# An adaLN transformer block with a ternary feed-forward on one core: the prologue's loads on two queues, first products by feature halves, and the last group's transpositions and gating reordered

## The chip, the cores and the metric

One core of one Trainium2 chip runs the whole block in one launch. The metric is the device time of one execution in microseconds (us), median over several runs.

## The reference

The input x holds 8 sequences of 128 tokens with 256 features, and a condition vector of 256 features belongs to each sequence. Everything is float32.

```python
ada = (cond @ ada_w + ada_b)[:, None, :]
shift1, scale1, gate1, shift2, scale2, gate2 = split(ada, 6)
x1 = ln(x) * (1 + scale1) + shift1
q, k, v = (x1 @ qkv_w + qkv_b)            # 16 heads of 128
attn = softmax(q k^T / sqrt(128)) v
x = x + gate1 * (attn @ out_w + out_b)
x2 = ln(x) * (1 + scale2) + shift2
x = x + gate2 * (gelu(x2 @ ffn_w1 + ffn_b1) @ ffn_w2 + ffn_b2)
# second block: two products with weights rounded to {-s, 0, s} by groups of 64
h = square(relu(x @ ternary(W_fc).T))
out = x_in + rms_norm(h) @ ternary(W_proj).T
```

`x_in` is the input of the kernel; the hidden width of both feed-forwards is 1024.

## The kernel before

**Tiling.** The eight sequences form two quads of four (512 tokens). Features lie on the partitions in two halves of 128 (`KD = 2`), so an activation tile is 128 x 512 and a matrix product is a series of TensorE instructions with 512 columns into one PSUM bank of eight. For precision each float32 operand is split into a high part and a low part, and a product is three instructions: high by high, high by low, low by high (`split_mm`, L1225 to L1231). ScalarE (ACT) makes the high parts by a copy; VectorE (DVE) or GpSimd (POOL) make the low parts by a subtraction (`x_lo_part` L881, `lo_part` L348 to L350).

**Order of the work.** Every engine has its own instruction list, written out by hand, and the lists meet in counting semaphores. There is no planner. A list runs strictly in its order, so what stands behind a wait waits as well.

- *Prologue.* SP (the block at L289) loads x quad 0 in two halves (`x0_in`), the first part of ada_w, the first head's Q and K weights, four bias vectors, the V weights and the rest. ACT's queue loads the condition and ada_b (L664, L665). TensorE transposes the condition (L1433) and ada_b (L1436), fills waiting time with products of the identity (`keep_awake`, L1425 to L1427), makes the conditioning products (`ada_product`, L1438, L1442), and transposes the normalised quad 0 (`transpose_x`, L1446 to L1464, first quad at L1456) sequence by sequence and then raw x (`transpose_raw`, L1415 to L1423). DVE and ACT then modulate it out of PSUM: DVE feature half 1 (L868), ACT half 0 (L520), four sequences each. `first_query` makes Q of head 0 from the halves as they come, the biases are transposed at L1502, and K (`project`), the first V block (`first_values`, L1489 to L1498) and the scores (L1298) follow. Then come the products of the second head and the transposition of the normalised quad 1 (L1463).
- *Loop.* Sixteen heads in four groups (`NG`) of four; in a group a unit is one head of one quad, eight units (`UG`). For each unit TensorE makes scores, transposes the probabilities, multiplies by the values (`pv`) and by the output weights; DVE finds maxima, ACT takes exponentials, POOL normalises (L391). Projections of coming heads lie between.
- *Last group.* The units are written out (`last_unit` L1385 and DVE's `unit` with `last`). In unit 5 DVE adds the last output product of quad 0 to yT (`accumulate` L969), multiplies by the gate and adds x (`gate_y`, L958 to L967). In unit 6 TensorE transposes yT back (`transpose_y`, L1537 to L1543, instructions on L1541), and the second normalisation begins. Output head by head is split by ACT (`o_hi_part` L532) and DVE (`o_lo_part`, L949 to L953).
- *First feed-forward, quad 0* (L1607 to L1622 on TensorE, L728 to L733 on ACT, L1122 to L1131 on DVE). For each of eight hidden blocks c: TensorE `ffn1`, ACT GELU into one of two buffers (L718) and the high part, DVE the low part (`h_lo_part`, L893). A GELU waits until the low part two blocks earlier is made, since it writes over its buffer; `ffn1` waits for the GELU two blocks earlier, since it writes over its bank. Into this stretch fall quad 1's `accumulate` (L976), `gate_y` (L962, L966), `transpose_y`, the statistics for its normalisation (L814, L833) and the transpositions of the ternary weights (L1581). The second product of the feed-forward follows and in it the transposition of the normalised quad 1 (L1463).
- *Ternary feed-forward* and output at the end.

The wait that orders the transpositions of yT before the change:

```python
def transpose_y(quad):
    pe.wait_ge(gated, quad + 1)
    for s in range(SQ):
        for c in range(KD):
            m = nc.tensor.transpose(bank[BACK[quad][s // 2]][...], yT[:, c, cols(quad, s)], ident[:, :])
    m.then_inc(gt_mm, 1)
```

Of the kernel before, what the change touches and what calls it, by code (L numbers as in the profile page):

```python
# [21 lines left out]
P = 128  # L22
# [3 lines left out]
H = 16  # L26
# [31 lines left out]
def adaln_block(nc, x, cond, ada_w, ada_b, qkv_w, qkv_b, out_w, out_b, ffn_w1, ffn_b1, ffn_w2, ffn_b2,  # L58
                w_fc, w_proj, out):
    ctx = ExitStack()  # L60
    with ctx:
# [125 lines left out]
        x01_hi, xn0_done, xt0_done = sem("x01_hi"), sem("xn0_done"), sem("xt0_done")  # L187
# [152 lines left out]
        def _(pool):  # L340
# [124 lines left out]
            for k in range(KD):  # L465
                wv_lo_part(k, k + 1)
# [24 lines left out]
        def _(act):  # L491
# [15 lines left out]
            def modulate(e, shift, scale, src):  # L507

                quad, xf = e % NQ, xfull if e else xq0
                if e:  # L510
                    act.wait_ge(xt_done, e)
                act.wait_ge(ada_ready, 1 if e < NQ else 2)
                if e >= 1:
                    act.wait_ge(xs_lo, KD * e)
                for s in range(SQ):
                    b = quad * SQ + s
                    if e == 0:
                        act.wait_ge(xt0_done, s // 2 + 1)
                        src = bank[6:8] if s > 1 else (bank[BV], bank[BO])
                    m = nc.scalar.activation(xf[:, 0, s * P:(s + 1) * P], src[0][:, s * P:(s + 1) * P], ACT.Identity,  # L520
                                             bias=ada[:, shift, b:b + 1], scale=ada[:, scale, b:b + 1])
# [3 lines left out]
                if e:  # L525
                    act.wait_ge(mod_d, e + 1)
                    hi_part(x_hi[:, 1, cols(quad)], xfull[:, 1, :], xs_hi)
# [141 lines left out]
            nc.scalar.activation(bias[:, 0:NA], bank[6][:, 0:NA], ACT.Copy).then_inc(small_cp, 1)  # L669
# [5 lines left out]
            act.wait_ge(small_t, 3)  # L675
            nc.scalar.activation(bias[:, NA:NBIAS], bank[4][:, 0:NBIAS - NA], ACT.Copy).then_inc(small_cp, 1)
            nc.scalar.activation(kbias[:, :], bank[4][:, KB - NA:VB - NA], ACT.Copy, scale=SCALE).then_inc(small_cp, 1)
            act.wait_ge(small_cp, 4)
            wqk_hi_part(1, 32)
            keep_k0(0, 1)  # L680
# [120 lines left out]
        def _(dve):  # L801
# [53 lines left out]
            def modulate(e, shift, scale, src):  # L855

                quad, xf = e % NQ, xfull if e else xq0
                if e:
                    dve.wait_ge(xt_done, e)
                dve.wait_ge(ada_ready, 1 if e < NQ else 2)  # L860
                if e:
                    dve.wait_ge(xs_lo, KD * e)
                for s in range(SQ):
                    b = quad * SQ + s
                    if e == 0:
                        dve.wait_ge(xt0_done, s // 2 + 1)
                        src = bank[6:8] if s > 1 else (bank[BV], bank[BO])
# [4 lines left out]
                if e:  # L872
                    split_lo(quad, KD * e)
                else:
                    nc.vector.tensor_copy(x_hi[:, 1, cols(quad)], xf[:, 1, :]).then_inc(x01_hi, 1)
                    dve.wait_ge(x01_hi, 1)
                    x_lo_part(quad, 1, xf)
                    dve.wait_ge(xs_hi, 1)
# [851 lines left out]
```

## Time and profile before

| | us |
|---|---|
| median of 3 runs | 350.53 |
| lowest and highest run | 349.86, 351.02 |
| the profiled execution | 350.69 |
| its span, first to last instruction | 348.9 |
| TensorE busy | 342.3 |
| VectorE busy | 222.4 |
| ScalarE busy | 220.2 |
| GpSimd busy | 148.7 |

Busy times are sums over instructions in the span. PE is TensorE's products and PEld its weight loads, which overlap them; the end of a product is modelled, so the step from the start of one to the start of the next is the better measure of its cost. SPq and ACTq are the instruction queues of SP and ACT when they issue a transfer. The idle time before an instruction stands in square brackets with what released it.

### The profile page before, as it was taken

Reading aid. Unit: us, or ns where it says so; the run is one execution under the profiler, and the core shown is the slowest. Engines: PE = TensorE matmul, PEld = TensorE weight load, DVE = VectorE, ACT = ScalarE, POOL = GpSimd, SP = SyncE. Lnnn points to the kernel's source line nnn. Section 1 sums busy time; section 2 is a strip of 40 time slices with the busy share of each in tenths; the row PEclk is TensorE's granted clock in tenths of the full one; section 3 lists DMA queues with packets and bytes.
Section 4 is the critical chain, followed back from the end, with each engine's and each line's share of the span. In section 5 each row is a group of like instructions: output and inputs, shape, how many; then the busy total and the mean of one; then the engine's idle time right before and its main releaser. Section 6 shows DMA issues by size and latency. Waiting matters only on the chain.

```text
span 348.9 us, 5879 instructions
## 1 busy us (share of the span) xinstructions
PE 342.3 (98%) x1950; PEld 293.7 (84%) x1950; DVE 222.4 (64%) x386; ACT 220.2 (63%) x560; POOL 148.7 (43%) x140
## 2 busy tenths in 40 slices
PE   8999999999999999999999999999999999999995
PEld 7888888889888888888888888888787788889884
DVE  6676756553555664456466454585875788577796
ACT  2773565667576657756664675667579536876593
POOL 3571329736534964644595573479341100000000
PEclk9999999999999999999999999999999999999998
DMA  6953003100300320030020002020000000000002
GB/s 176 362 192 120 3 0 120 62 1 3 120 0 0 120 60 0 0 120 0 25 95 0 0 6 115 0 62 0 4 0 2 0 2 0 0 2 1 1 32 90
DMA packets 12338, 16.53 MB, mean 47 GB/s; under 512 B 720, under 2 KB 8992, under 8 KB 12320
## 3 DMA queue, kind: packets, MB, share of 16 engines
q1 hardware_dynamic: 12136, 16.16, 14.2%
q8 instruction: 10, 0.16, 0.2%
q10 hardware_dynamic: 184, 0.15, 0.1%
q14 instruction: 8, 0.07, 0.1%
HBM read 15.25 MB, written 1.05 MB: 47 GB/s over the span
## 4 chain that ended last, share of the span: by engine, by line
PE 74%; issue 20%; DVE 3%; ACT 1%; POOL 1%; POOLq 0%; ACTq 0%
PE bank L1228 16%; PE bank L1230 16%; PE bank L1229 16%; PE bank L1315 8%; PE bank L1298 8%; PE bank L1304 4%; PE bank L1427 2%; PE bank L1442 1%; DVE yT L976 1%; DVE yT L966 1%; PE bank L1463 1%; PE bank L1422 1%; DVE yT L962 0%; ACT prob L579 0%; ACT hbuf L718 0%
## 5 line engine op out<-in xcount | busy, mean ns | idle before, releaser
L391 POOL TENSOR_TENSOR prob<-prob,rinv 128x512 f32<-128x512 f32 x32 | 36.2, 1131 | 60.3 <-DVE rinv L1025 59.9
L579 ACT ACTIVATE prob<-bank,negmax 128x128 f32<-128x128 f32 x128 | 45.4, 365 | 25.6 <-DVE negmax L1012 25.6
L1315 PEld LDWEIGHTS bank<-probT,vals 128*128 128x128 f32 x256 | 33.3, 191 | 3.2 <-issue 0.8
L952 DVE SCALAR_TENSOR_TENSOR o_lo<-bank,bias,o_hi 128x512 fp32r<-128x512 f32 x32 | 23.9, 745 | 17.2 <-ACT o_hi L532 17.2
L532 ACT ACTIVATE o_hi<-bank,bias 128x512 fp32r<-128x512 f32 x32 | 21.9, 686 | 19.4 <-PE bank L1315 19.4
L1315 PE MATMUL bank<-probT,vals 128*128 128x128 f32 x256 | 33.9, 275 | 0.0
L350 POOL TENSOR_TENSOR wqk_lo<-raw_qk,wqk_hi 128x512 fp32r<-128x512 f32 x16 | 21.2, 1323 | 19.6 <-ACT wqk_hi L493 18.1
L488 POOL TENSOR_TENSOR xr<-raw_qk,xt 128x256 f32<-128x256 f32 x1 | 0.7, 721 | 67.2 <-ACT raw_qk L796 67.2
L1012 DVE TENSOR_REDUCE negmax<-bank 128x4 f32<-128x512 f32 x32 | 21.8, 682 | 7.9 <-PE bank L1298 7.9
L1228 PE MATMUL bank<-wv_hi,x_hi 128*128 128x512 f32 x62 | 26.1, 420 | 0.0
L579 ACT ACTIVATION_READ_ACCUMULATOR prob<-bank,negmax 128x1 f32 x128 | 26.0, 203 | 0.0
L1025 DVE RECIPROCAL rinv<-rowsum 128x4 f32<-128x4 f32 x32 | 5.7, 177 | 31.2 <-ACT prob L579 31.2
L1228 PE MATMUL bank<-o_hi,wo_hi 128*128 128x512 f32 x64 | 25.3, 395 | 0.0
L1230 PE MATMUL bank<-o_hi,wo_lo 128*128 128x512 f32 x64 | 25.0, 390 | 0.0
L1229 PE MATMUL bank<-o_lo,wo_hi 128*128 128x512 f32 x64 | 24.9, 390 | 0.0
L1230 PE MATMUL bank<-wv_hi,x_lo 128*128 128x512 f32 x62 | 24.4, 393 | 0.0
L1229 PE MATMUL bank<-wv_lo,x_hi 128*128 128x512 f32 x62 | 24.2, 390 | 0.0
L1228 PE MATMUL bank<-x_hi,wqk_hi 128*128 128x512 f32 x54 | 24.0, 445 | 0.0
L537 ACT ACTIVATE vals<-bank 128x512 f32<-128x512 f32 x32 | 19.0, 601 | 4.5 <-PE bank L1230 3.4
L1230 PE MATMUL bank<-x_hi,wqk_lo 128*128 128x512 f32 x54 | 21.2, 393 | 0.0
L1229 PE MATMUL bank<-x_lo,wqk_hi 128*128 128x512 f32 x54 | 21.1, 392 | 0.0
L897 DVE COPY probT<-bank 128x512 f32<-128x512 f32 x29 | 19.8, 683 | 2.0 <-PE bank L1304 2.0
(218 smaller groups left out, 974.1 us busy)
## 6 DMA issues: line engine op xcount, KB each, us to landing
raw_qk<-in_L_cond_qkv_w_dram SPq DMA_DIRECT2D x6, 512.0 KB, 4.6
raw_v<-in_L_cond_qkv_w_dram SPq DMA_DIRECT2D x4, 512.0 KB, 4.1
raw_o<-in_L_cond_out_w_dram SPq DMA_DIRECT2D x4, 512.0 KB, 3.5
t_w<-in_L_cond_ada_w_dram SPq DMA_DIRECT2D x1, 1024.0 KB, 8.9
raw_w<-in_L_cond_ffn_w_dram SPq DMA_DIRECT2D x2, 512.0 KB, 6.9
t_raw<-in_L_ffn_W_fc_dram SPq DMA_DIRECT2D x4, 256.0 KB, 3.7
t_raw<-in_L_ffn_W_proj_dram SPq DMA_DIRECT2D x4, 256.0 KB, 3.8
raw_qk<-in_L_cond_ffn_w_dram SPq DMA_DIRECT2D x1, 1024.0 KB, 4.9
```

The costliest lines, as they stand in the source:

```text
L350: nc.gpsimd.tensor_tensor(lo, raw, hi.bitcast(F32), ALU.subtract).then_inc(lo_sem, 1)
L391: nc.gpsimd.tensor_tensor(e, e, rinv[:, j % 2, :].unsqueeze(2).broadcast_to([P, SQ, P]), ALU.mult).then_inc(norm_done, 1)
L532: nc.scalar.activation(hi, psum, ACT.Identity, bias=bias[:, bass.ds(at, 1)]).then_inc(hi_sem, 1)
L579: e = nc.scalar.activation(prob[:, j % 2, s, :], bank[BS][:, s * P:(s + 1) * P], ACT.Exp, bias=negmax[:, j % 2, s:s + 1], accum_out=rowsum ...
L897: nc.vector.tensor_copy(probT[:, :, :].rearrange("p s t -> p (s t)"), bank[BV][:, :]).then_inc(p_done, 1)
L952: nc.vector.scalar_tensor_tensor(out=lo[:, :], in0=bank[BO][:, :], scalar=bias[:, bass.ds(HG * G + VB + j % HG, 1)], in1=hi[:, :].bitcast( ...
L1012: nc.vector.tensor_reduce(negmax[:, j % 2, :], bank[BS][:, :].rearrange("p (s t) -> p s t", s=SQ), axis=AX.X, op=ALU.max, negate=True).the ...
L1228: nc.tensor.matmul(dst, ah, bh, start=start and n == 0, stop=False, skip_group_check=True)
L1229: nc.tensor.matmul(dst, ah, bl, start=False, stop=False, skip_group_check=True)
L1230: m = nc.tensor.matmul(dst, al, bh, start=False, stop=stop and n == len(terms) - 1, skip_group_check=True)
L1298: m = nc.tensor.matmul(bank[BS][:, t], q[:, t], k[:, t], start=True, stop=True)
L1315: m = nc.tensor.matmul(bank[BO][:, s * P:(s + 1) * P], vals[:, b, h], probT[:, s, :], start=True, stop=True)
```

## The change

In the prologue the second half of x quad 0 and the four bias vectors are loaded from ACT's queue, the half of x first of all, and SP waits for the first half of x alone. The biases are transposed together with ada_b into one bank, ahead of the conditioning products, and copied in one go. There are 5, 3 and 1 calls of `keep_awake` where there were 5, 7 and 3, and they stand elsewhere. The first quad is transposed by feature half, half 1 first; both DVE and ACT modulate both halves, DVE sequences 0 and 1, ACT sequences 2 and 3, and each makes the high part of its own two sequences. Q and K of head 0 are made together from the halves. One wv_lo part moves from POOL to DVE, and DVE copies one half of the transposed raw x (`xT`) that ACT copied; ACT's half comes later. In the last group `gate_y` is cut in two (`gate_y` and `add_x`) with a signal for each feature half, and yT is transposed by halves. In the first feed-forward of quad 0, gate and add of quad 1 stand behind low parts 2 and 3, the statistics behind low part 6 instead of 5, and the transposition of yT behind hidden block 6 instead of 5.

```diff
 @block.sync
-            for h in range(2):
-                s = slice(h * SQ // 2, (h + 1) * SQ // 2)
-                sp.dma_start(xt[:, s, :], x[s].rearrange("b t d -> t b d")).then_inc(x0_in[h], 16)
+            sp.dma_start(xt[:, 0:SQ // 2, :], x[0:SQ // 2].rearrange("b t d -> t b d")).then_inc(x0_in[0], 16)
             sp.dma_start(ada_w1, ada_w[:, 0:2 * D].rearrange("(k p) n -> p k n", p=P)).then_inc(ada1_in, 16)
-            sp.wait_ge(x0_in[1], 16)
+            sp.wait_ge(x0_in[0], 16)
...
-            for src, at, n in ((qkv_b, QB, 3 * H), (out_b, OB, KD), (ffn_b1, F1B, NC), (ffn_b2, F2B, KD)):
-                sp.dma_start(brow[at - NA:at - NA + n, :], src.rearrange("(n p) -> n p", p=P)).then_inc(bias_in, 16)
 @block.gpsimd
             pool.wait_ge(xs_lo, KD)
-            for k in range(KD):
-                wv_lo_part(k, k + 1)
+            wv_lo_part(0, 1)
 @block.scalar
+            def modulate_first():
+                act.wait_ge(ada_ready, 1)
+                for k, src, full, hi in ((1, bank[7], m1_a, hi1_a), (0, bank[6], mod_a, xs_hi)):
+                    act.wait_ge(xt0_done, KD - k)
+                    for b in range(SQ // 2, SQ):
+                        m = nc.scalar.activation(xq0[:, k, b * P:(b + 1) * P], src[:, b * P:(b + 1) * P], ACT.Identity,
+                                                 bias=ada[:, SHIFT1 + k, b:b + 1], scale=ada[:, SCALE1 + k, b:b + 1])
+                    m.then_inc(full, 1)
+                    act.wait_ge(full, 1)
+                    hi_part(x_hi[:, k, SQ // 2 * P:SQ * P], xq0[:, k, SQ // 2 * P:SQ * P], hi)
...
+            act.dma_start(xt[:, SQ // 2:SQ, :], x[SQ // 2:SQ].rearrange("b t d -> t b d")).then_inc(x0_in[1], 16)
             act.dma_start(crow, cond).then_inc(cond_in, 16)
             act.dma_start(arow, ada_b.rearrange("(n p) -> n p", p=P)).then_inc(arow_in, 16)
+            for src, at, n in ((qkv_b, QB, 3 * H), (out_b, OB, KD), (ffn_b1, F1B, NC), (ffn_b2, F2B, KD)):
+                act.dma_start(brow[at - NA:at - NA + n, :], src.rearrange("(n p) -> n p", p=P)).then_inc(bias_in, 16)
...
-            modulate(0, SHIFT1, SCALE1, bank[0:2])
+            modulate_first()
             for k in range(KD):
                 wkeep_v(k, 16)
-            copy_xT(0, (bank[BE], bank[BS]))
...
+            act.wait_ge(small_cp, 3)
+            keep_k0(0, 1)
             wqk_hi_part(1, 32)
-            keep_k0(0, 1)
+            act.wait_ge(xraw_mm, 1)
+            nc.scalar.activation(xT[:, 0, cols(0)], bank[BE][:, :], ACT.Copy).then_inc(xT_done, 1)
             wqk_hi_part(2, 32)
 @block.vector
+            def modulate_first():
...
+                dve.wait_ge(hi1_d, 1)
+                dve.wait_ge(hi1_a, 1)
+                x_lo_part(0, 1, xq0)
+                dve.wait_ge(hi0_d, 1)
+                dve.wait_ge(xs_hi, 1)
+                x_lo_part(0, 0, xq0)
...
+            def add_x(quad):
                 dve.wait_ge(xT_done, quad + 1)
+                dve.wait_ge(xT1_done, 1)
                 for c in range(KD):
                     dve.wait_ge(gate_mul, KD * quad + c + 1)
-                    m = nc.vector.tensor_tensor(yT[:, c, cols(quad)], yT[:, c, cols(quad)], xT[:, c, cols(quad)], ALU.add)
-                m.then_inc(gated, 1)
+                    nc.vector.tensor_tensor(yT[:, c, cols(quad)], yT[:, c, cols(quad)], xT[:, c, cols(quad)], ALU.add).then_inc(gated, 1)
...
-            modulate(0, SHIFT1, SCALE1, bank[0:2])
-            dve.wait_ge(small_cp, 4)
+            modulate_first()
+            dve.wait_ge(wv_h, 2)
+            nc.vector.tensor_tensor(wv_lo[:, 1, :], raw_v[:, 1, :], wv_hi[:, 1, :].bitcast(F32), ALU.subtract).then_inc(wv_l, 1)
+            dve.wait_ge(xraw_mm, 1)
+            nc.vector.tensor_copy(xT[:, 1, cols(0)], bank[BS][:, :]).then_inc(xT1_done, 1)
+            dve.wait_ge(small_cp, 3)
             keep_q0(0, 0, 1)
...
                 h_lo_part(0, c)
                 if c == 1:
                     accumulate(NU - 1, NG - 1, 1, last=True)
+                if c == 2:
                     gate_y(1)
-                if c == 5:
+                if c == 3:
+                    add_x(1)
+                if c == 6:
                     dve.wait_ge(gt_mm, 2)
                     stats_of(3)
 @block.tensor
+            keep_awake(3)
             pe.wait_ge(arow_in, 16)
-            nc.tensor.transpose(bank[6][:, 0:NA], arow, ident[0:NA, 0:NA]).then_inc(small_t, 1)
+            nc.tensor.transpose(bank[6][:, 0:NA], arow, ident[0:NA, 0:NA])
+            pe.wait_ge(bias_in, 64)
+            nc.tensor.transpose(bank[6][:, NA:NBIAS], brow, ident[0:NBIAS - NA, 0:NBIAS - NA]).then_inc(small_t, 1)
...
-            keep_awake(7)
-            pe.wait_ge(small_cp, 2)
+            keep_awake(1)
+            pe.wait_ge(small_cp, 1)
             pe.wait_ge(ada1_in, 16)
             ada_product(0, GATE1, ada_w1, bank[5])
             transpose_x(0, bank[0:2])
             pe.wait_ge(ada_ready, 1)
             transpose_raw(0, (bank[BE], bank[BS]))
-            keep_awake(3)
...
+                for k in (1, 0):
...
+                    for w in (wqk_hi, wqk_lo):
+                        if w is wqk_lo:
+                            pe.wait_ge(wqk_l, 1)
+                        for n in range(2):
+                            nc.tensor.matmul(dsts[n][:, :], w[:, n * KD + k, 0:P], x_hi[:, k, cols(0)],
+                                             start=k == 1 and w is wqk_hi, stop=False)
...
-            first_query()
-            pe.wait_ge(bias_in, 64)
-            nc.tensor.transpose(bank[4][:, 0:NBIAS - NA], brow, ident[0:NBIAS - NA, 0:NBIAS - NA]).then_inc(small_t, 1)
-            project(bank[BK], 1, 0, 0).then_inc(k_mm, 1)
+            first_qk()
             first_values()
-            pe.wait_ge(small_cp, 4)
-            pe.wait_ge(xT_done, 1)
+            pe.wait_ge(xT1_done, 1)
             scores(0, 0)
...
             def transpose_y(quad):
-                pe.wait_ge(gated, quad + 1)
-                for s in range(SQ):
-                    for c in range(KD):
+                for c in range(KD):
+                    pe.wait_ge(gated, KD * quad + c + 1)
+                    for s in range(SQ):
...
-                if c == 5:
+                if c == 6:
                     pe.wait_ge(xT_done, 2)
                     transpose_y(1)
-                if c == 6:
                     pe.wait_ge(t_done, NG)
                     pe.wait_ge(ident_set, 2)
                     transpose_fc(0)
```

## Rows read from the trace of the kernel before

**Rows 1.** The page, first section: busy time, share of the span, instructions.
```profile
PE 342.3 (98%) x1950; PEld 293.7 (84%) x1950; DVE 222.4 (64%) x386; ACT 220.2 (63%) x560; POOL 148.7 (43%) x140
```

**Rows 2.** The timeline, TensorE, 4 to 12: start, duration, engine, line, operation, tiles.
```profile
4.38 3.35 PE L1427 MATMUL bank<-ident 128*128 128x128 f32 x14
7.52 2.22 PE L1442 MATMUL bank<-condT,hbuf 128*128 128x8 f32 x16
9.60 1.07 PE L1456 MATMUL bank<-ident,prob 128*128 128x128 f32 x8
...
11.38 0.83 PE L1427 MATMUL bank<-ident 128*128 128x128 f32 x6
```

**Rows 3.** The timeline, issues of transfers on both queues, 0 to 6.
```profile
0.73 0.95 SPq L293 DMA_DIRECT2D xt<-in_x_dram  x2
0.73 0.62 ACTq L664 DMA_DIRECT2D t_up<-in_cond_dram  x1
...
5.15 0.46 SPq L299 DMA_DIRECT2D t_up<-in_L_cond_qkv_b_dram  x1
```

**Rows 4.** The timeline, VectorE, ScalarE and GpSimd, 10 to 20.
```profile
10.34 1.50 ACT L520 ACTIVATE xq<-bank,ada 128x128 f32<-128x128 f32 x4 [2.10 <-PE bank L1456]
10.34 1.37 DVE L868 TENSOR_SCALAR xq<-bank,ada 128x128 f32<-128x128 f32 x4 [0.30 <-PE bank L1456]
...
12.21 1.29 DVE L882 TENSOR_TENSOR x_lo<-xq,x_hi 128x512 fp32r<-128x512 f32 x2
...
12.41 1.14 ACT L493 ACTIVATE wv_hi<-raw_v 128x512 fp32r<-128x512 f32 x2
...
14.73 0.75 DVE L900 TENSOR_SCALAR qT<-bank,bias 128x512 f32<-128x512 f32 x1 [1.23 <-ACT kbias L677]
...
16.07 1.30 POOL L350 TENSOR_TENSOR wqk_lo<-raw_qk,wqk_hi 128x512 fp32r<-128x512 f32 x1
...
18.84 1.38 DVE L833 TENSOR_SCALAR xn<-xt,mv,rstd 128x256 f32<-128x256 f32 x4
```

**Rows 5.** The timeline, TensorE, from the second quad's transpositions.
```profile
20.66 1.03 PE L1463 MATMUL bank<-ident,xn 128*128 128x128 f32 x8
...
21.45 0.48 PE L1228 MATMUL bank<-wv_hi,x_hi 128*128 128x512 f32 x1
```

**Rows 6.** The timeline, TensorE and VectorE, last group, 247 to 255.
```profile
247.08 1.28 DVE L966 TENSOR_TENSOR yT<-yT,xr 128x512 f32<-128x512 f32 x2
...
248.50 1.06 PE L1541 MATMUL bank<-ident,yT 128*128 128x128 f32 x8 [0.40 <-DVE yT L966]
...
249.32 0.48 PE L1228 MATMUL bank<-x_hi,wqk_hi 128*128 128x512 f32 x1
...
253.44 0.75 DVE L952 SCALAR_TENSOR_TENSOR o_lo<-bank,bias,o_hi 128x512 fp32r<-128x512 f32 x1 [0.35 <-ACT o_hi L532]
...
254.31 0.48 PE L1228 MATMUL bank<-o_hi,wo_hi 128*128 128x512 f32 x1
```

**Rows 7.** The timeline, first feed-forward of quad 0, 270 to 283.
```profile
270.02 1.29 DVE L966 TENSOR_TENSOR yT<-yT,xr 128x512 f32<-128x512 f32 x2
...
271.02 0.39 PE L1230 MATMUL bank<-x_hi,w_lo 128*128 128x512 f32 x1
271.22 1.29 DVE L893 TENSOR_TENSOR hid_lo<-hbuf,hid_hi 128x512 fp32r<-128x512 f32 x2
271.46 1.07 PE L1541 MATMUL bank<-ident,yT 128*128 128x128 f32 x8
272.00 0.69 ACT L718 ACTIVATE hbuf<-bank,bias 128x512 f32<-128x512 f32 x1 [1.91 <-DVE hid_lo L893]
...
272.74 0.50 PE L1228 MATMUL bank<-x_hi,w_hi 128*128 128x512 f32 x1 [0.22 <-ACT hbuf L718]
...
278.88 1.90 DVE L833 TENSOR_SCALAR raw_qk<-bank,mv,rstd 128x256 f32<-128x256 f32 x4
...
282.04 1.04 PE L1463 MATMUL bank<-ident,raw_qk 128*128 128x128 f32 x8
```

More of the change, by code:

```diff
@@ L871, in modulate @@
                 dve.wait_ge(mod_d, e + 1)
[L872 to L878, printed above, removed]
-                    x_lo_part(quad, 0, xf)
+                split_lo(quad, KD * e)
+            def modulate_first():
+                dve.wait_ge(ada_ready, 1)
+                for k, src, full, hi in ((1, bank[BO], m1_d, hi1_d), (0, bank[BV], mod_d, hi0_d)):
+                    dve.wait_ge(xt0_done, KD - k)
+                    for b in range(SQ // 2):
+                        m = nc.vector.tensor_scalar(xq0[:, k, b * P:(b + 1) * P], src[:, b * P:(b + 1) * P],
+                                                    ada[:, SCALE1 + k, b:b + 1], ada[:, SHIFT1 + k, b:b + 1], ALU.mult, ALU.add)
+                    m.then_inc(full, 1)
+                    dve.wait_ge(full, 1)
+                    nc.vector.tensor_copy(x_hi[:, k, 0:SQ // 2 * P], xq0[:, k, 0:SQ // 2 * P]).then_inc(hi, 1)
+                dve.wait_ge(hi1_d, 1)
[4 more added lines that the diff above has]
+                x_lo_part(0, 0, xq0)
             def x_lo_part(quad, k, xf=xfull):
@@ L1448, in transpose_x @@
                 if e == 0:
-                    for s in range(SQ):
-                        if s < SQ - 1:
-                            pe.wait_ge(xn0_done, s + 1)
-                        else:
-                            pe.wait_ge(xn_done, 1)
-                        dst = bank[6:8] if s > 1 else (bank[BV], bank[BO])
-                        for k in range(KD):
+                    pe.wait_ge(small_cp, 3)
+                    for k in (1, 0):
+                        for s in range(SQ):
+                            if s < SQ - 1:
+                                pe.wait_ge(xn0_done, s + 1)
+                            else:
+                                pe.wait_ge(xn_done, 1)
+                            dst = bank[6:8] if s > 1 else (bank[BV], bank[BO])
                             m = nc.tensor.transpose(dst[k][:, s * P:(s + 1) * P], src[:, s, k * P:(k + 1) * P], ident[:, :])
-                        if s % 2:
-                            m.then_inc(xt0_done, 1)
+                        m.then_inc(xt0_done, 1)
                     return
@@ L1472, in _, with first_qk @@
             transpose_raw(0, (bank[BE], bank[BS]))
-            keep_awake(3)
-            def first_query():
+            def first_qk():
+                dsts = (bank[BQ], bank[BK])
                 pe.wait_ge(wqk_h, 1)
-                for k, ready in ((1, x01_hi), (0, xs_hi)):
-                    pe.wait_ge(ready, 1)
-                    nc.tensor.matmul(bank[BQ][:, :], wqk_hi[:, k, 0:P], x_hi[:, k, cols(0)], start=k == 1, stop=False)
-                pe.wait_ge(wqk_l, 1)
                 for k in (1, 0):
-                    nc.tensor.matmul(bank[BQ][:, :], wqk_lo[:, k, 0:P], x_hi[:, k, cols(0)], start=False, stop=False)
-                for n, k in enumerate((1, 0)):
-                    pe.wait_ge(xs_lo, n + 1)
-                    m = nc.tensor.matmul(bank[BQ][:, :], wqk_hi[:, k, 0:P], x_lo[:, k, cols(0)], start=False, stop=k == 0)
-                m.then_inc(q_mm, 1)
+                    if k:
+                        pe.wait_ge(hi1_d, 1)
+                        pe.wait_ge(hi1_a, 1)
+                    else:
+                        pe.wait_ge(hi0_d, 1)
+                        pe.wait_ge(xs_hi, 1)
+                    for w in (wqk_hi, wqk_lo):
[4 more added lines that the diff above has]
+                                             start=k == 1 and w is wqk_hi, stop=False)
+                for k in (1, 0):
+                    pe.wait_ge(xs_lo, KD - k)
+                    for n, done in ((0, q_mm), (1, k_mm)):
+                        m = nc.tensor.matmul(dsts[n][:, :], wqk_hi[:, n * KD + k, 0:P], x_lo[:, k, cols(0)], start=False, stop=k == 0)
+                        if k == 0:
+                            m.then_inc(done, 1)
             def first_values():
@@ L1537, in transpose_y @@
             def transpose_y(quad):
-                pe.wait_ge(gated, quad + 1)
-                for s in range(SQ):
-                    for c in range(KD):
+                for c in range(KD):
+                    pe.wait_ge(gated, KD * quad + c + 1)
+                    for s in range(SQ):
                         m = nc.tensor.transpose(bank[BACK[quad][s // 2]][:, (s % 2) * D + c * P:(s % 2) * D + (c + 1) * P],
```

43 lines of the change are left out of this document (16 added, 27 removed).

## The prediction

> **What bounds the kernel now.** The page's first section is read first: TensorE is busy for 98% of the span and no other engine for more than 64% [rows 1]. TensorE is the bound. So an edit pays only if a product that the rest of TensorE's list waits for starts earlier, or if a stall in that list closes. VectorE or ScalarE work that gets shorter elsewhere is worth nothing. The timeline, read for TensorE alone, then shows where it is busy without being useful: the prologue, and two waits in the last group and the first feed-forward.
>
> In the prologue TensorE fills its time with identity products (L1427). Their rows say one thing more. Fourteen of them start at 4.38 and are followed at 7.52, some 0.22 each, but six at 11.38 take 0.83, of which the last alone is about 0.28: 0.11 each from start to start [rows 2]. The same instruction on the same tile runs at half the rate early on: TensorE is at the lower of its two levels (1.2 GHz) there and at 2.4 GHz by 11.38, though the clock column of the page shows no drop in these slices. The sixteen conditioning products (L1442) lie across the change: they start at 7.52 and the transpositions follow at 9.60 [rows 2]. Taking n of them at 0.22 and 16 - n at 0.11 for these 2.08 us gives n = 3, so the rate doubles about 8.2 us into the span.
>
> After the prologue the products hang on a chain over the other engines: modulation starts at 10.34, the copy of Q at 14.73, the second quad is normalised until 20.22, and TensorE transposes it from 20.66 [rows 4, 5]. That is late by hardly more than the handover, so whatever gains time on TensorE before that point is lost again unless the normalisation is earlier too.
>
> **The change part by part: loads.** The second half of x moves to ACT's queue, which issued its first transfer at 0.73 and needs 0.6 for it; on SP the pair took 0.95 [rows 3]. So ada_w is issued some 0.45 earlier. The condition vector now stands behind 256 KB of x on ACT's queue. I put it at 4.1 instead of before 3.96, where its transposition starts now. Four bias transfers go to ACT too; the one shown took 0.46 to issue [rows 3], so at up to 0.46 each they end by about 3.7, and ScalarE's table load moves behind them. Only condT waits for that, and it is wanted at 6.6. SP in turn is free of them, and raw_v, the other Q/K weights and the second quad of x start over 1.5 earlier. None of these was the last thing waited for, so I cost that at nothing. The cover is the modulation chain.
>
> **Start of the conditioning products.** Condition transposed at 4.1 to 4.4, three filler calls (six instructions) for 1.3 at the low rate until 5.7, arow and the 60 bias rows (the old L1502 moved up, 0.3 with its handover) until 6.0, one filler call for 0.44: with the handover conditioning starts at 6.6 instead of 7.52, and 0.9 is gained. But it is gained at the low rate. From 6.6 to 8.2, 7.3 of the sixteen products fit, and the other 8.7 take 0.96: transpositions follow at 9.15 instead of 9.60. So **0.45, not 0.9**, reaches them, and the modulation starts at 9.9. The half order (all four sequences of feature half 1 first) leaves four transpositions before the first modulation, as before.
>
> **Modulation to Q.** Before, 14.73 - 10.34 = 4.39 lie between the two. After, ScalarE does two blocks (0.75, half of the 1.50), a half copy (0.35), and both again: 2.3 with handovers, then both wv_hi copies, 1.14: 3.5 [rows 4]. VectorE then makes wv_lo for one half (0.65, as x_lo), copies raw x out of PSUM (0.65), and only then copies Q: 4.8 after the start. That is 0.4 longer, because two operations were moved onto VectorE ahead of the copy of Q. Start 0.45 earlier and chain 0.4 longer leave Q at about 14.68, and the normalisation at 20.17. Q and K together end on TensorE about 1.3 earlier, but scores wait for the copy of Q, and then the second head's products wait for wqk_lo, which POOL makes in 1.30 from 16.07 now [rows 4] and from some 15.8 then. So TensorE stands for part of what it won. Its next stand is the normalised second quad: in the last group transpositions begin 0.14 after their VectorE operation ends and the next product 0.82 after that [rows 6]. 20.17 + 0.96 is 21.13, and this product stands at 21.45 now [rows 5]. **The prologue gives 0.32.** Bounds: nothing, if the condition or the biases land 0.4 later, and 0.8, if the rate doubles after 10 in both kernels, since then the whole 0.9 arrives.
>
> **Last group, quad 0.** Adding x half by half lets four transpositions begin on the first half. Now the pair of additions from 247.08 ends at 248.36 and the transpositions start at 248.50 [rows 6]; one addition earlier they start near 247.95 and end 0.4 sooner. I cost this at nothing: the next thing TensorE waits for is the low part of head output 5, which VectorE makes from 253.44 to 254.19, and the product stands at 254.31 [rows 6], 0.12 after it. That operation hangs on ScalarE's exponentials and not on TensorE, and its chain is the same. The cover gone, the 0.4 would be gained.
>
> **First feed-forward, quad 1.** Here the last product before the transpositions starts at 271.02, so the next could at 271.25; it starts at 271.46, since the additions end at 271.31. The next product starts at 272.74, 1.28 later where 0.82 was enough: it waits for a GELU that could only begin at 272.00, because VectorE made the low part it needs from 271.22, behind accumulate, gate and add, six operations in a row, of which the additions stand in [rows 7]. That is 0.21 + 0.46 = 0.67 of stall. After, the gate stands behind low part 2 and the add behind low part 3, so low part 2 is ready near 269.6 and low part 3 near 271.4; the GELUs at 270.1 and 271.5 follow the products. The transpositions go behind product 6 (near 272.6), when the first half has been added (272.1) and the second nearly (272.7). Standing next to the ternary transpositions they save one change between transposition and product too, some 0.08. **This gives 0.75.** Late next is the fourth normalisation: VectorE's statistics start 0.1 later, so it ends near 280.9 (280.78 now [rows 7]), and TensorE, 0.75 earlier than 282.04 [rows 7], wants it at 281.3. Nothing to pay, with 0.4 to spare. Bounds: 0.4, if the statistics come one low part (0.65) later, which would eat the 0.4 and 0.3 more, and 0.75.
>
> **Sum.** 0.32 + 0 + 0.75 = 1.07 off the profiled execution's 350.69 (span 348.9) is 349.6. That execution lies 0.16 above the median of the runs, 350.53; taken off the median the forecast is 349.5.
>
> **A rule against it.** The six filler products at 11.38 are gone, and of fifteen calls nine are left. By the Trainium skill (TensorE: Matmul & The Clock Gate, Part 1) the throttled state is the default and recent activity releases it; by that rule work taken out of the first microseconds may hold the low rate longer. No row shows what the conditioning products are worth for the release; the trace agrees that the rise came after an unbroken run of work.
>
> **The rivals.**
> *The rate doubles later than 8.2* because TensorE does less in the first 8 us. If it doubled only near 12, all sixteen products would take 3.5 (to 10.1), modulation would start four transpositions of 0.22 and a handover later, near 11.1, Q would be copied at 15.9, 1.2 later than now, and the product after the normalised quad would stand at 21.13 + 1.2 = 22.3: 0.9 lost, 0.7 won in the tail, 350.7. If it doubled at 15.5, the first Q and K products would start at 13.6 after all sixteen transpositions; four would run at twice the 0.23 of a product of 512 columns and eight at 0.23, to 17.3. Q would be copied then, 2.5 later than now, and the product would stand near 23.6: 2.2 lost, less 0.7, 352.0. It is slower at all from a doubling near 12, and measurably from near 14. For it: the fillers taken out, and a new gap before the bias rows. Against it: TensorE still works almost without a break from 4.4 to 8.2. 15% in all, 9% for the late form, the only one here that is slower by more than can be told.
> *The tail gives less:* low parts 4 to 7 run behind the add, and the fourth normalisation or the ternary weight copies come late; half of the 0.75 is given back and the prologue gives 0.1: 350.1. For it: the add now stands ahead of low part 4. Against it: the 0.4 to spare. 18%.
> *More than the sum:* the rise comes late or early by its own chance in each execution and the prologue's 0.9 arrives whole: 348.9. 14%.
> *The change does not do what it says:* both queues feed the same transfer capacity, x arrives no sooner, ada_w neither, and fillers stand where they stood: prologue 0, tail 0.75, 349.8. 3%.
> My forecast keeps 50%.
>
> **How the numbers follow.** 0.3% of 350.53 is 1.05 us, about what a measurement of this kernel can tell from no change: below 349.48 is faster, above 351.58 slower. My sum of 1.07 ends right on the bound, so the forecast's 50% split, 31 faster and 19 same: what I cost at nothing (earlier loads, quad 0's transpositions) can only add. With the 14 of "more", faster is 0.45. Same is these 19, the short tail's 18, the unmoved loads' 3 and 6 for the mild clock case: 0.46. Slower is the late clock case: 0.09. The range runs from 348.5 ("more", and quad 0's 0.4 with it) to 350.8 (the mild clock case).
>
> **What would show it.** L1442 starting near 6.6 and the transpositions near 9.15; a change of spacing from 0.22 to 0.11 inside L1442; the copy of Q near 14.7 and xn at 20.2; a short TensorE gap before the second head's products; in the last group the yT transpositions in two fours and a new gap before the product at 254.3; no gap between feed-forward products 5 and 6. It is wrong if the spacing of 0.22 goes on into the transpositions, if Q's copy comes earlier than 14.4, or if TensorE gaps stay at GELU 4.

## The result and the profile after

The changed kernel takes 352.45 us, the median of five runs (352.31 to 353.12), against 349.88 (349.86 to 351.02) for the kernel before in the same session: a ratio of 1.0068 with the interval [1.0052, 1.0084]. It is **slower** by 2.4 us by the ratio, 2.6 from median to median, where 1.07 less was forecast, and it lies outside the range of 348.5 to 350.8. The profiled execution took 352.31. The two profiled executions are only 1.6 apart, since that of the kernel before, 350.69, was 0.8 above its median.

The page of the kernel after, its span and its busy line:

```profile
span 350.5 us, 5859 instructions
...
PE 343.6 (98%) x1938; PEld 295.2 (84%) x1938; DVE 224.5 (64%) x389; ACT 220.0 (63%) x559; POOL 147.6 (42%) x139
```

This is the page of before almost to the digit [rows 1]: the span is 1.6 longer (348.9 before), and no share tells why. A TensorE that works slowly counts as busy as one that works fast.

The timeline of after, TensorE alone (start, duration of the group, engine, line, operation, tiles, shape, count, and in brackets the idle time before with what ended it):

```profile
4.32 0.38 PE L1453 MATMUL bank<-ident,t_up 8*128 8x8 f32 x2 [0.30 <-DMA t_up<-in_cond_dram]
4.63 1.65 PE L1447 MATMUL bank<-ident 128*128 128x128 f32 x6
6.27 0.28 PE L1457 MATMUL bank<-ident,t_up 12*128 12x12 f32 x1
6.68 0.36 PE L1459 MATMUL bank<-ident,t_up 60*128 60x60 f32 x1
6.97 0.79 PE L1447 MATMUL bank<-ident 128*128 128x128 f32 x2
7.55 3.42 PE L1465 MATMUL bank<-condT,hbuf 128*128 128x8 f32 x16
10.83 1.95 PE L1480 MATMUL bank<-ident,prob 128*128 128x128 f32 x8
12.57 1.92 PE L1442 MATMUL bank<-ident,xt 128*128 128x128 f32 x8
14.13 1.04 PE L1512 MATMUL bank<-x_hi,wqk_hi 128*128 128x512 f32 x2
15.01 0.63 PE L1512 MATMUL bank<-x_hi,wqk_lo 128*128 128x512 f32 x2
...
20.19 0.50 PE L1248 MATMUL bank<-x_hi,wqk_hi 128*128 128x512 f32 x1 [0.45 <-POOL wqk_lo L347]
...
23.07 1.10 PE L1486 MATMUL bank<-ident,xn 128*128 128x128 f32 x8
23.92 0.48 PE L1248 MATMUL bank<-wv_hi,x_hi 128*128 128x512 f32 x1
```

Read it against [rows 2, 5]. The conditioning products start at 7.55, where before had 7.52, so the order of work brought nothing there. They then take 3.28 to the transpositions where before took 2.08: all sixteen at 0.21, none at 0.11. The eight transpositions behind them take 1.74, 0.22 each, twice the 0.11 that [rows 2] have for such tiles at the high rate. Only in the first Q and K products does the spacing change: the first pair is followed 0.88 later, the second pair runs at the 0.23 of one product. So TensorE stays at the lower of its two levels, 1.2 GHz, until near 14.8 us, not 8.2. The product after the second quad's transpositions stands at 23.92, 2.47 after the 21.45 of [rows 5], where 21.13 was forecast.

Two of the loads issued from ScalarE's queue, timeline of after:

```profile
0.74 0.50 ACTq L666 DMA_DIRECT2D xt<-in_x_dram  x1
...
1.92 0.30 ACTq L668 DMA_DIRECT2D t_up<-in_L_cond_ada_b_dram  x1
```

and, of after too, what TensorE's idle time ahead of the small transpositions ended with (us and times, the weight load and the product each counted):

```profile
its engine sat idle before it (us, times) until:
  DMA t_up<-in_cond_dram: 0.9, 2
  DMA t_up<-in_L_cond_ada_b_dram: 0.3, 1
  DMA t_up<-in_L_cond_ffn_b_dram: 0.2, 1
```

Each of the three groups of small transpositions (condition, ada_b, biases) now waits for its own load. ada_b is 6 KB, issued at 1.92 behind a half of x. Its transposition starts at 6.27, and at 4.2 in the kernel before, but six fillers stand in front of it and hide most of that.

The other engines of after, timeline:

```profile
12.03 0.73 DVE L879 TENSOR_SCALAR xq<-bank,ada 128x128 f32<-128x128 f32 x2 [0.76 <-PE bank L1480]
...
15.34 1.29 POOL L347 TENSOR_TENSOR wv_lo<-raw_v,wv_hi 128x512 fp32r<-128x512 f32 x1 [6.05 <-DVE x_lo L892]
15.50 1.67 DVE L1082 TENSOR_TENSOR wv_lo<-raw_v,wv_hi 128x512 fp32r<-128x512 f32 x1 [0.25 <-ACT wv_hi L489]
...
17.57 0.69 ACT L544 ACTIVATE kT<-bank,kbias 128x512 f32<-128x512 f32 x1 [2.10 <-issue]
17.70 0.73 DVE L910 TENSOR_SCALAR qT<-bank,bias 128x512 f32<-128x512 f32 x1
18.16 0.62 ACT L489 ACTIVATE wqk_hi<-raw_qk 128x512 fp32r<-128x512 f32 x1
18.86 1.27 POOL L347 TENSOR_TENSOR wqk_lo<-raw_qk,wqk_hi 128x512 fp32r<-128x512 f32 x1 [2.23 <-ACT wqk_hi L489]
...
21.63 1.38 DVE L837 TENSOR_SCALAR xn<-xt,mv,rstd 128x256 f32<-128x256 f32 x4 [0.89 <-issue]
```

From modulation to the copy of Q lie 17.70 - 12.03 = 5.67, where [rows 4] have 4.39 and the forecast had 4.8. VectorE's half of wv_lo, costed at 0.65, took 1.67: it began 0.16 after POOL had begun the other half, and ended 0.54 after POOL's 16.63. By the Trainium skill (SBUF — State Buffer, "SBUF: two separate sides") a VectorE operation with two SBUF inputs and a GpSimd operation that reads SBUF exclude each other: whichever starts first holds the shared ports for its whole length. The row agrees with that: the 0.54 left behind POOL's end is about the 0.65 that such an operation takes alone. Further down ScalarE copies K at 17.57 and only then makes the second head's high part at 18.16, so POOL's low part runs until 20.13 and TensorE stands for 0.45 ahead of 20.19. The normalised second quad is ready at 21.63 + 1.38 = 23.01, and its transpositions follow at 23.07.

The end of the kernel after, timeline of TensorE:

```profile
251.33 0.47 PE L1248 MATMUL bank<-x_hi,wqk_hi 128*128 128x512 f32 x1
...
256.75 0.50 PE L1248 MATMUL bank<-o_hi,wo_hi 128*128 128x512 f32 x1 [0.18 <-DVE o_lo L962]
...
275.01 1.03 PE L1570 MATMUL bank<-ident,yT 128*128 128x128 f32 x8
...
283.65 1.03 PE L1486 MATMUL bank<-ident,raw_qk 128*128 128x128 f32 x8
```

The 2.47 lost in the prologue are 2.01 at 251.33 (249.32 before), for the halves of quad 0 gain 0.46 there, and 2.44 again at 256.75 (254.31 before), behind a new gap that the low part of head output 5 ends [rows 6]. At 283.65 the kernel is 1.61 behind the 282.04 of [rows 7]: the feed-forward part gave 0.83, where 0.75 was forecast, and 1.6 is what the span shows. **In the profiled executions the whole error lies in the first 24 us.**

### The profile page after: what moved, and what is told of

It is laid out like the page before. It is cut to its first block, busy times and chain, and to the rows that moved or that the text cites. A ratio compares the mean times of both kernels' runs of the same rounds, so it can differ in the third digit from the quotient of the medians.

```text
span 350.5 us, 5859 instructions
## 1 busy us (share of the span) xinstructions
PE 343.6 (98%) x1938; PEld 295.2 (84%) x1938; DVE 224.5 (64%) x389; ACT 220.0 (63%) x559; POOL 147.6 (42%) x139
## 3 DMA queue, kind: packets, MB, share of 16 engines
HBM read 15.25 MB, written 1.05 MB: 46 GB/s over the span
## 4 chain that ended last, share of the span: by engine, by line
PE 68%; issue 20%; ACT 4%; DVE 4%; DMA 1%; POOL 1%; ACTq 1%; POOLq 0%
PE bank L1248 16%; PE bank L1250 15%; PE bank L1249 15%; PE bank L1335 8%; PE bank L1318 7%; PE bank L1324 4%; PE bank L1465 2%; DMA t_up<-in_L_cond_ffn_b_dram 1%; ACT prob L581 1%; DVE hid_lo L903 1%; PE bank L1442 1%; DVE yT L979 1%; ACT hbuf L722 1%; DVE o_lo L962 1%; ACT o_hi L534 1%
## 5 line engine op out<-in xcount | busy, mean ns | idle before, releaser
L1248 PE MATMUL bank<-x_hi,wqk_hi 128*128 128x512 f32 x52 | 23.2, 445 | 0.4 <-POOL wqk_lo L347 0.4
L1250 PE MATMUL bank<-x_hi,wqk_lo 128*128 128x512 f32 x52 | 20.4, 393 | 0.0
```

Source lines behind the costliest of these rows:

```text
L1248: nc.tensor.matmul(dst, ah, bh, start=start and n == 0, stop=False, skip_group_check=True)
L1250: m = nc.tensor.matmul(dst, al, bh, start=False, stop=stop and n == len(terms) - 1, skip_group_check=True)
```

## The experiments

Two theories stood after the result. **Clock**: fewer filler products ahead of conditioning leave TensorE at 1.2 GHz for longer, and the first 15 us are worked at half speed. **Chain**: the loads behind x and the operations moved onto VectorE and ScalarE make Q late whatever the clock does. All of these kernels compute the whole reference. Each ratio is to the kernel before in the same session, whose medians were 350.17, 350.21 and 350.05.

**Only the last group's part** (all of the diff's edits to gate, add, yT's transpositions and statistics, on the kernel before).

```diff
+            def add_x(quad):
...
+                if c == 2:
                     gate_y(1)
+                if c == 3:
+                    add_x(1)
+                if c == 6:
```

> The kernel before with the last-group and feed-forward part of the change alone (transpositions of yT by halves, gate and add behind low parts 2 and 3). Theory: the two stalls of TensorE around the transpositions of quad 1 go (0.7 to 0.85 us) and nothing else moves, so 0.7 to 0.9 us faster than before. Rival, that the changed kernel's loss lies partly in this part: 0.3 us faster at most, or slower.

Measured: 349.19 (348.58 to 349.72, 12 runs), ratio 0.9973 [0.9962, 0.9984]. This part is faster by 0.27%, 0.95 us, and it is the best version of the study, ahead of both kernels. Its profiled execution is shorter by more (span 347.5), but some 0.45 of that is not this part's: there the rate had doubled before the conditioning products (timeline, TensorE), and the transpositions stand at 9.15.

```profile
7.44 1.85 PE L1447 MATMUL bank<-condT,hbuf 128*128 128x8 f32 x16
```

**Only the prologue's part** (the changed kernel with those edits undone).

> The changed kernel with the last-group and feed-forward part undone. Theory: the whole loss is the prologue's, so it is 0.7 to 0.9 us slower than the changed kernel, some 2.4 us over the profiled execution of before. Rival: equal to the changed kernel.

Measured: 353.38 (353.20 to 354.28, 5 runs), 1.0102 [1.0085, 1.0120]: slower by 3.2 us from median to median, by 3.6 from the ratio. Less the 0.95 that the other part gains, this is 2.3 to 2.6, and the whole change measured 2.4: the parts add up.

**Three filler calls fewer, nothing else**, on the kernel before.

```diff
-            keep_awake(7)
+            keep_awake(4)
```

> The kernel before with 4 filler calls instead of 7 ahead of the conditioning products; nothing else differs. Clock theory: the conditioning products start near 6.6 instead of 7.5 but the spacing of 0.21 us goes on past 8.2, to 11 or later, and the kernel is 0.5 to 2 us slower than before. Rival (the loads and the longer chain on VectorE cause the loss, the clock follows its own time and still rises near 8.2): 0.3 to 0.5 us faster.

Measured: 352.70 (350.80 to 352.99, 6 runs, one at 350.8), 1.0065 [1.0045, 1.0085]. Its timeline, TensorE:

```profile
4.38 2.08 PE L1427 MATMUL bank<-ident 128*128 128x128 f32 x8
6.62 3.55 PE L1442 MATMUL bank<-condT,hbuf 128*128 128x8 f32 x16 [0.17 <-DMA hbuf<-in_L_cond_ada_w_dram]
10.02 1.95 PE L1456 MATMUL bank<-ident,prob 128*128 128x128 f32 x8
...
13.47 1.11 PE L1427 MATMUL bank<-ident 128*128 128x128 f32 x6
```

The experiment that decides most. Conditioning starts 0.90 earlier than in [rows 2], just what the change set out to do, and the transpositions follow 0.42 *later*: the spacing stays at 0.21 until the fillers at 13.47. With no load, no order and no operation of another engine touched, this is 2.5 us slower from median to median, 2.3 by the ratio. What the forecast wanted from the prologue did not come even with the loads in time: the one execution at 350.8 is no faster than the kernel before either.

**Fillers put back into the change**, so that conditioning starts still later than it does.

```diff
-            keep_awake(3)
+            keep_awake(6)
...
-            keep_awake(1)
+            keep_awake(2)
```

> The changed kernel with 6 filler calls in place of 3 ahead of ada_b's transposition and 2 in place of 1 ahead of the conditioning products. Clock theory: the spacing halves near 7 to 8.5 as before, conditioning starts later (8.2 to 8.5) but ends near 10.3 instead of 11, and the kernel is 0.8 to 1.5 us faster than the changed one. Rival (the late biases and the longer chain on the other engines cause the loss): conditioning later by 0.8, so up to 0.8 us slower than the changed kernel.

Measured: 351.35 (351.31 to 351.63, 7 runs), 1.0035 [1.0023, 1.0046]. Timeline, TensorE:

```profile
4.78 2.93 PE L1447 MATMUL bank<-ident 128*128 128x128 f32 x12
...
8.73 1.85 PE L1465 MATMUL bank<-condT,hbuf 128*128 128x8 f32 x16
10.44 1.07 PE L1480 MATMUL bank<-ident,prob 128*128 128x128 f32 x8
...
23.08 0.48 PE L1248 MATMUL bank<-wv_hi,x_hi 128*128 128x512 f32 x1
```

and VectorE:

```profile
11.18 0.73 DVE L879 TENSOR_SCALAR xq<-bank,ada 128x128 f32<-128x128 f32 x2 [0.30 <-PE bank L1480]
...
16.86 0.74 DVE L910 TENSOR_SCALAR qT<-bank,bias 128x512 f32<-128x512 f32 x1
```

Conditioning starts 1.18 later than in the changed kernel and the transpositions 0.39 earlier, since all sixteen products run at 0.11. So the earlier rate, less what the later start costs, is worth about 1.1 us, half of the loss. What is left at 23.08 are 1.63 in two parts. From transpositions to the product behind the second quad lie 12.64, against 11.85 in [rows 2, 5] at the same rate: 0.79 more, the chain's. The transpositions themselves stand 0.84 later than before's 9.60, because conditioning starts later. From modulation to the copy of Q lie 5.68, as in the changed kernel, so that stretch is not the clock's.

**The second head's weights ahead of the copy of K** on ScalarE, since wqk_lo ends a stall of 0.45 at 20.19.

```diff
-            keep_k0(0, 1)
             wqk_hi_part(1, 32)
+            keep_k0(0, 1)
```

> The changed kernel with ScalarE making the second head's high parts ahead of the copy of K again. The wait of TensorE for wqk_lo (0.45 us before the second head's products) goes. If that wait decides, 0.4 us faster than the changed kernel; if the normalisation of the second quad, which ends just as TensorE asks for it, decides, within 0.1 us of it.

Measured: 352.35 (352.24 to 352.93, 4 runs), 1.0061 [1.0042, 1.0079], the same as the change, as was expected if the normalisation decides. The stall at the second head is gone, but the timeline shows where it went:

```profile
23.77 1.10 PE L1486 MATMUL bank<-ident,xn 128*128 128x128 f32 x8 [0.27 <-DVE xn L837]
```

TensorE waits for the normalised second quad instead. In this execution the rate doubled only near 16.8, which delays the copy of Q as well, so the run alone does not price the order. But the changed kernel's own rows say the same: its second quad is normalised at 23.01 and transposed from 23.07, so a stall closed ahead of that has nothing to gain. An early stall in front of a later one is worth nothing.

**The same, with VectorE's half of wv_lo back on POOL.**

```diff
-            wv_lo_part(0, 1)
+            for k in range(KD):
+                wv_lo_part(k, k + 1)
...
-            dve.wait_ge(wv_h, 2)
-            nc.vector.tensor_tensor(wv_lo[:, 1, :], raw_v[:, 1, :], wv_hi[:, 1, :].bitcast(F32), ALU.subtract).then_inc(wv_l, 1)
```

> As after_order, and the low part of the second V weight half back on GpSimd. VectorE's subtraction of 1.67 us beside GpSimd's goes, the copy of Q and the normalisation come 1 us or more earlier, and TensorE then waits for neither: 0.4 to 0.9 us faster than the changed kernel. If the clock alone causes the loss: within 0.2 us of it.

Measured: 352.39 (351.33 to 352.86, 5 runs), 1.0057 [1.0038, 1.0076]. A miss: 0.4 to 0.9 less than the changed kernel was expected, and it equals it, which the expectation had given to the clock alone. The profiled execution shows why the times do not decide: the rate doubled near 16.2, later than in the changed kernel, and the copy of Q waited for TensorE's slow products and not for VectorE:

```profile
18.02 0.75 DVE L911 TENSOR_SCALAR qT<-bank,bias 128x512 f32<-128x512 f32 x1 [2.10 <-PE bank L1516]
```

**All three edits together**: fillers, order and POOL.

> The changed kernel with the more fillers, the order on ScalarE and the V low part on GpSimd together. If clock and chain are separate causes the two gains add: 1.3 to 2.3 us faster than the changed kernel, so 350 to 351; whether it beats before with the tail alone (349.2) is doubtful: at best equal.

Measured: median 353.76 of 350.01, 350.29, 353.52, 354.00, 354.19 and 354.20, ratio 1.0087 [1.0053, 1.0122]. By its median a miss (350 to 351 was expected). There are two groups of executions of one program, over 3 us apart with nothing between. The profiled execution is the one at 350.01, where the rate doubled at 7.5. Its timeline, TensorE, and then VectorE:

```profile
8.32 1.85 PE L1464 MATMUL bank<-condT,hbuf 128*128 128x8 f32 x16
10.03 1.07 PE L1479 MATMUL bank<-ident,prob 128*128 128x128 f32 x8
...
21.70 0.47 PE L1247 MATMUL bank<-wv_hi,x_hi 128*128 128x512 f32 x1
```

```profile
10.77 0.73 DVE L880 TENSOR_SCALAR xq<-bank,ada 128x128 f32<-128x128 f32 x2 [0.30 <-PE bank L1479]
...
15.28 0.75 DVE L911 TENSOR_SCALAR qT<-bank,bias 128x512 f32<-128x512 f32 x1 [0.69 <-PE bank L1516]
```

Modulation to Q is 4.51 where the change has 5.67, and transpositions to product 11.67 where the chain as changed has 12.64. Order and POOL together give back 0.97 at equal rate, which the run before could not show. Even so its executions at 350.0 and 350.3 do not reach the 349.2 of the last group's part alone.

**Fillers moved among the conditioning products**: as many before them as in the four-call kernel, and one call behind each of the first three chunks.

```diff
+                    if w is ada_w1 and c < GATE1 - 1:
+                        keep_awake(1)
...
-            keep_awake(7)
+            keep_awake(4)
```

> The kernel before with all its 15 filler calls, but 4 ahead of the conditioning products and 3 between them (one after each of the first three chunks), so that conditioning begins near 6.6 and TensorE does the same instructions in another order. If it is the fillers' number in the stretch ahead of 8.2 that brings the high rate, they are nearly all still there: spacing halves near 8, time within 0.4 us of before. If it is the early start of conditioning that keeps the rate low, it stays low until 11 or later and the kernel is 1.5 to 2.5 us slower, as with 4 calls.

Measured: 353.43 (350.18 to 353.85, 10 runs, three of them at 350.2 to 351.3), 1.0077 [1.0051, 1.0103]. Timeline, TensorE:

```profile
6.42 0.99 PE L1442 MATMUL bank<-condT,hbuf 128*128 128x8 f32 x4
7.27 0.78 PE L1427 MATMUL bank<-ident 128*128 128x128 f32 x2
...
14.45 0.83 PE L1427 MATMUL bank<-ident 128*128 128x128 f32 x6
```

The same number of fillers as before, without a gap, and in the profiled execution still slow until 14.3. Seven of ten executions are over 3 us above the kernel before, which is more than was expected; the three others are within 1.3 us of it. So it is not the fillers' number alone: where they stand, all ahead of the conditioning products, matters in most executions.

**Condition and ada_b ahead of x** on ScalarE's queue, in the changed kernel.

```diff
-            act.dma_start(xt[:, SQ // 2:SQ, :], ...
             act.dma_start(crow, cond).then_inc(cond_in, 16)
             act.dma_start(arow, ...
+            act.dma_start(xt[:, SQ // 2:SQ, :], ...
```

> The changed kernel with ACT's queue issuing the condition and ada_b ahead of the half of x. Load theory (ada_b lands at 6.2 because it stands behind 256 KB of x): ada_b lands near 4, the condition near 2.7, and conditioning starts 0.3 to 0.5 earlier. Clock theory: this brings nothing in time as long as the rate stays low until 14 to 15: within 0.4 us of the changed kernel.

Measured: 353.50 (352.27 to 353.84, 4 runs), 1.0086 [1.0064, 1.0107]. A miss: 1.05 above the changed kernel, where 0.4 at most was expected. Timeline, TensorE:

```profile
5.84 0.28 PE L1457 MATMUL bank<-ident,t_up 12*128 12x12 f32 x1
7.83 0.36 PE L1459 MATMUL bank<-ident,t_up 60*128 60x60 f32 x1 [1.71 <-DMA t_up<-in_L_cond_ffn_b_dram]
...
8.70 3.42 PE L1465 MATMUL bank<-condT,hbuf 128*128 128x8 f32 x16
```

ada_b no longer holds anything up, but the four bias transfers, still behind x, land 1.1 later than in the change, and conditioning starts at 8.70. Whichever small load stands behind x on that queue is the late one. The rate doubled later too in this execution, near 17.0, so the 1.05 is not the price of the loads alone.

**Only x's halves on two queues**, on the kernel before.

```diff
+            act.dma_start(xt[:, SQ // 2:SQ, :], x[SQ // 2:SQ].rearrange("b t d -> t b d")).then_inc(x0_in[1], 16)
             act.dma_start(crow, cond).then_inc(cond_in, 16)
...
-            sp.wait_ge(x0_in[1], 16)
+            sp.wait_ge(x0_in[0], 16)
```

> The kernel before with the second half of x first on ACT's queue, and SP waiting for the first half alone: the load part of the change by itself (biases stay on SP). Load theory: the condition lands near 4.2 and ada_b near 6, where TensorE waits for it ahead of its seven filler calls, so these end near 9.3 and conditioning starts 1.5 to 2 later: 1 to 2 us slower than before. Rival (x and ada_w earlier help, ada_b is not late by itself): within 0.3 us or faster.

Measured: 353.86 (352.09 to 355.93, 4 runs), 1.0116 [1.0064, 1.0168]. Timeline, TensorE:

```profile
6.39 0.28 PE L1435 MATMUL bank<-ident,t_up 12*128 12x12 f32 x1 [1.73 <-DMA t_up<-in_L_cond_ada_b_dram]
6.60 3.35 PE L1426 MATMUL bank<-ident 128*128 128x128 f32 x14
9.75 2.23 PE L1441 MATMUL bank<-condT,hbuf 128*128 128x8 f32 x16
```

In the order of the kernel before, all fourteen fillers stand behind ada_b's transposition. It waits for 1.73, and conditioning starts 2.23 later than in [rows 2]. The fillers in front of the bias rows in the changed kernel hide most of this wait. The span is 2.2 longer than before's, more than the 1 to 2 expected. The four timed runs lie 3.8 above by their median but are spread over as much, so the price of this edit is known to lie between 2 and 6 us and no better.

## Why the prediction was wrong

**The bound, right.** TensorE bounds the kernel, an early gain counts only if it reaches the product behind the second quad, and what is lost there is carried to the end: 2.47 at 23.92, 1.6 in the span once the tail had won 0.83.

**The rate doubles near 8.2 as before: the step that failed first.** It doubled near 14.8. The forecast took the moment of the doubling as fixed, whatever work stood ahead of it, and gave the rival that moved it 15%. Against the forecast the low rate cost 0.73 on the conditioning products (3.28 against the 2.55 put from 6.6; the kernel before, from 7.52, took 2.08) and 0.45 behind them (13.09 from transpositions to product, 12.64 with the fillers back). The reason offered against the rival, that TensorE still worked almost without a break from 4.4 to 8.2, was no evidence: the spread-filler kernel works without a break too and stays slow. Nor is a gap the cause: the changed kernel stands 0.30 ahead of 4.32, but the one with more fillers stands 0.44 at the same place and doubles near 8.3. The rival's late form had priced the right thing: doubling at 15.5, product near 23.6, 352.0; measured 14.8, 23.92 and 352.45. That it comes so close is in part luck, for it too starts conditioning at 6.6, 0.95 too early, and doubles 0.7 too late.

**Conditioning at 6.6: wrong by 0.95.** The fillers start at 4.63 instead of 4.4, as the condition came later (0.23). From there to ada_b's transposition lie 1.64 instead of 1.3, and from that to the next filler 0.70 instead of 0.3; the last step is as put. Waiting for ada_b and the biases is the smaller part of these 0.74. In the kernel with more fillers only the condition is waited for, and yet 0.35 pass from the last filler to ada_b's transposition and 0.49 from there to the next filler, against 0.41 and 0.70 here. So the late loads cost 0.23 + 0.06 + 0.21 = 0.50; the other 0.45 are steps between unlike instructions, which the sum had put too short. The forecast looked at the condition's landing behind 256 KB and at the *issue* of the biases ("by about 3.7"), and never asked when ada_b and the biases would land. Its bound "nothing, if the condition or the biases land 0.4 later" was the right worry. That the earlier loads "can only add" was wrong too: the statistics of x's first half start at 3.88, in the kernel before at 3.49, and the load part alone made the kernel slower by 2 us or more. Four fillers, with the loads as before and no bias rows among them, did start conditioning at 6.62, and that gained nothing.

**Modulation to Q, 4.8: wrong by 0.87.** The term is wv_lo on VectorE, 0.65 put and 1.67 measured, taken from an x_lo that ran with POOL idle. The order of the additions was right. The path is as long at the high rate, 5.68 with more fillers; with this operation back on POOL it is 4.51.

**Stands of TensorE, right in place.** "A short gap before the second head's products" is the 0.45 at 20.19. With it removed, TensorE waited for the normalisation, the very next stand that the text had named.

**Quad 0 at nothing, right.** The halves gained 0.46 at 251.33 and the low part of head output 5 took it back at 256.75, with the new gap that was forecast.

**Feed-forward, 0.75: right.** 0.83 in the profiled execution; the last group's and this part together gave 0.95 by twelve runs of their own. No wait for the fourth normalisation came.

**The sum.** The product stood at 23.92 against 21.13: 0.95 for the late start, 0.73 and 0.45 for the clock, 0.66 for the chain, together 2.79. The 0.66 are 12.64 less the 11.98 that the forecast had. The sizes belong to this order of events; they are no independent prices, since an earlier start alone would have been eaten by the clock.

**What stays open.** Why the same program finds the high rate early in some executions and late in others (350.0 and 354.2), and which property of the work sets it. In the profiled executions, twelve or fourteen fillers in a row begun before 5 us went with a doubling at 7.3 to 8.3, fourteen begun at 6.6 with one at 10.5, and six or eight with 14 to 17; but the kernel with two groups of executions had twelve, and one of six executions with eight fillers, and three of ten with the fillers spread, came near the time of the kernel before. That the clock makes these groups is shown only for the executions that were profiled. No run has the changed prologue with all small loads ahead of x, so what the loads cost in it is known from the trace alone.

## What to carry to other kernels

Filler work that looks idle may be what brings the high rate early; before useful work is pulled forward over it, price the case that the rate rises later, and run that one edit by itself. Small loads that TensorE waits for do not belong behind a large one on a queue: ask when each lands, not when it is issued. A duration for an operation that is moved to another engine has to come from a row where its new neighbours are running too.

## What was not expected of the hardware

In the profiled executions of the changed kernel and of the one with four filler calls, the sixteen conditioning products, back to back for 3.3 us, were not followed by the high rate; it came only behind the sixteen transpositions that follow them. Begun 0.9 earlier, they made the kernel slower by 2.5 us. The Trainium skill (TensorE: Matmul & The Clock Gate, Part 1) holds the throttled state for the default that activity releases, which these runs bear out; its estimate that the ramp costs under 1% of a typical span is not contradicted by the 0.7% that the later rise cost with four filler calls, but that is over twice the change's hoped-for gain.

The clock column of the page reads 9 in every slice of the changed kernel, through more than 10 us at half rate. Only the spacing of equal instructions showed it.

A transfer of 6 KB issued at 1.92 behind 256 KB on the same queue was waited for until 6.4 in the kernel where only x moved; issued at 1.40 with x on the other queue it had been used by 4.2 us.
